# Attention kernel: the units of each batch's third block of row maxima are dealt out two steps ahead of that block's scores in place of one

## The reference, cut to what matters

```python
def _mhsa(X, ln_g, ln_b, Wq, bq, Wk, bk, Wv, bv, Wo, bo):     # X: (2, 1024, 256)
    Xn = (X - mu) * jax.lax.rsqrt(var + EPS) * ln_g + ln_b
    Q = split_heads(Xn @ Wq + bq)                             # 16 heads of 16
    K = split_heads(Xn @ Wk + bk)
    V = split_heads(Xn @ Wv + bv)
    scores = jnp.einsum('bhqd,bhkd->bhqk', Q, K) / jnp.sqrt(jnp.float32(D_HEAD))
    scores = jnp.where(causal, scores, jnp.float32(-jnp.inf))
    A = jax.nn.softmax(scores, axis=-1)
    AV = jnp.einsum('bhqk,bhkd->bhqd', A, V)
    ...
    return AV @ Wo + bo
...
x = _layernorm(x + attention(x))
x = _layernorm(x + mixture(x))    # softmax over 8 of U V x, weights from relu(x W1 + b1) W2 + b2
```

## Time and profile before

| | before |
|---|---|
| median of three runs | 435.47 us |
| lowest, highest | 435.21, 435.81 us |
| the profiled execution's own time | 435.95 us |
| its span, first to last instruction | 434.2 us |
| granted TensorE clock, mean | 0.995 |
| TensorE matmul, busy | 407.1 us (94%) |
| VectorE, busy | 309.1 us (71%) |
| ScalarE, busy | 243.3 us (56%) |
| GpSimd, busy | 74.6 us (17%) |

### The profile page before, as it was taken

One profiled execution on the slowest core, in us unless ns is written; L12 is line 12 of the kernel. 1 busy time (PEld: TensorE's weight loads), 2 busy tenths in 40 slices (PEclk: granted clock), 3 DMA queues, 4 the chain that ended last, 5 costly groups with the idle time before them and its releaser, 6 DMA issues.

```text
span 434.2 us, 7411 instructions
## 1 busy us (share of the span) xinstructions
PE 407.1 (94%) x2563; PEld 214.5 (49%) x2563; DVE 309.1 (71%) x811; ACT 243.3 (56%) x541; POOL 74.6 (17%) x111
## 2 busy tenths in 40 slices
PE   7998899999989989999999999999999998998994
PEld 3545444344333445466768734344334344556783
DVE  5538997798799766528488799789889863214665
ACT  6681555676767666543441265666676857542321
POOL 4430211143121010102230022114212011010000
PEclk9999999999999999999999999999999999999989
DMA  6166760450402000001764045054130000000011
GB/s 194 15 104 93 193 99 15 68 82 7 70 2 98 1 3 0 2 1 31 147 124 64 15 86 91 10 87 63 23 53 3 0 4 0 2 0 2 0 48 49
DMA packets 18452, 21.14 MB, mean 49 GB/s; under 512 B 4976, under 2 KB 11888, under 8 KB 18416
## 3 DMA queue, kind: packets, MB, share of 16 engines
q1 hardware_dynamic: 18365, 20.66, 25.4%
q10 hardware_dynamic: 51, 0.01, 0.0%
HBM read 5.79 MB, written 2.10 MB: 18 GB/s over the span
## 4 chain that ended last, share of the span: by engine, by line
PE 74%; DVE 16%; ACT 6%; issue 2%; DMA 1%; POOL 1%; ACTq 0%; DVEq 0%; POOLq 0%
PE ps L951 17%; PE ps L1066 14%; PE ps L1045 14%; PE ps L1022 10%; DVE mx L822 9%; PE ps L959 8%; PE ps L967 4%; PE ps L942 2%; PE ps L1026 2%; ACT pr L675 2%; PE ps L1136 2%; PE ps L1076 1%; DVE ps L818 1%; ACT stk L596 1%; ACT qk_raw L661 1%
## 5 line engine op out<-in xcount | busy, mean ns | idle before, releaser
L675 ACT ACTIVATE pr<-ps 128x512 f32<-128x512 f32 (+3 forms) x384 | 165.9, 495 | 95.5 <-PE ps L1045 94.0
L822 DVE TENSOR_REDUCE mx<-ps 128x1 f32<-128x512 f32 (+3 forms) x240 | 145.6, 665 | 14.6 <-PE ps L1022 7.4
L1045 PE MATMUL ps<-stq,stk 99*128 99x512 bf16 (+3 forms) x384 | 116.2, 330 | 4.6 <-ACT pr L675 3.3
L1022 PE MATMUL ps<-stk,stq 96*128 96x512 bf16 (+3 forms) x384 | 112.8, 327 | 2.1 <-DVE mx L822 0.9
L587 POOL TENSOR_SCALAR_AFFINE_SELECT pr<-pr 128x512 f32<-128x512 f32 x64 | 40.9, 639 | 253.6 <-ACT pr L675 253.6
L1066 PE MATMUL ps<-pr,va 128*32 128x512 f32 (+3 forms) x768 | 81.8, 498 | 0.0
L1045 PEld LDWEIGHTS ps<-stq,stk 99*128 99x128 bf16 x384 | 34.4, 98 | 90.4 <-ACT pr L675 51.8
L1022 PEld LDWEIGHTS ps<-stk,stq 96*128 96x128 bf16 x384 | 37.5, 98 | 23.5 <-issue 7.7
L818 DVE CUSTOM_DVE_ANT_0 ps<-ps,causal 128x384 f32<-128x384 f32 (+1 forms) x64 | 38.6, 646 | 11.3 <-PE ps L1022 11.3
L1026 PE MATMUL ps<-mask,ident_b 128*128 128x128 bf16 x192 | 35.4, 219 | 0.0
L951 PE MATMUL ps<-u_t,avt 128*128 128x256 f32 x128 | 30.8, 383 | 0.3 <-ACT avt L711 0.2
(11 more groups left out here) (108 smaller groups left out, 389.3 us busy)
## 6 DMA issues: line engine op xcount, KB each, us to landing
stq<-qk_raw SPq DMA_DIRECT2D x32, 96.0 KB, 2.8
stk<-qk_raw SPq DMA_DIRECT2D x32, 96.0 KB, 2.8
x_in<-in_x SPq DMA_DIRECT2D x8, 256.0 KB, 3.5
stq<-qk_raw SPq DMA_DIRECT2D x32, 64.0 KB, 2.4
stk<-qk_raw SPq DMA_DIRECT2D x32, 64.0 KB, 2.4
out_y<-x SPq DMA_DIRECT2D x3, 512.0 KB, 3.0
stk<-qk_raw SPq DMA_DIRECT2D x32, 32.0 KB, 2.4
stq<-qk_raw SPq DMA_DIRECT2D x32, 32.0 KB, 2.1
```

The costliest lines, as they stand in the source:

```text
L675: nc.scalar.activation(probs(b, g, s)[:, j, q0 - c * CHUNK:], act_bank(ev)[:, q0 - c * CHUNK:], ACT.Exp, scale=DH ** -0.5).then_inc(s_act_ ...
L822: nc.vector.tensor_reduce(dst, src, AX.X, ALU.max).then_inc(s_dve_free, 1)
L1022: last = nc.tensor.matmul(bank[:, i * w:(i + 1) * w], q[0:ROWS, t // TPC, j, tile(t % TPC)], k[0:ROWS, k0 // CHUNK, j, 0:w], start=True, s ...
L1045: nc.tensor.matmul(bank[:, q0 - c * CHUNK:], stk[stack_of(b, g)][0:ROWS + PARTS, kt // TPC, j, tile(kt % TPC)], stq[stack_of(b, g)][0:ROWS ...
```

## The change

One number: the third point of the course moves from one step ahead of the third block's first score to two, so from step 7 to step 6. The number of units due there (50) and the last point (step 37, 152 units) stay.

```diff
-    course = [(0, needed[0] + 6), (first_step[1], needed[1] + 12), (first_step[2] - 1, needed[2] + 1), (first_step[-1] - 3, needed[-1])]
+    course = [(0, needed[0] + 6), (first_step[1], needed[1] + 12), (first_step[2] - 2, needed[2] + 1), (first_step[-1] - 3, needed[-1])]
```

## The result

| | before | changed |
|---|---|---|
| median, taken side by side, 16 runs each | 436.03 us | 439.26 us |
| ratio to before, 95% interval | | 1.0065 (1.0042 to 1.0089) |
| profiled execution's own time, span | 435.95, 434.2 | 440.27, 438.2 |
| TensorE, VectorE, ScalarE busy in the profile | 407.1, 309.1, 243.3 | 410.6, 308.6, 243.9 |
| mean granted TensorE clock in the profile | 0.995 | 0.990 |

The change makes the kernel 0.65% slower: 2.8 us by the ratio (its interval is 1.8 to 3.9 us), 3.2 us between the two medians, and 4.0 us between the two profiled executions. The forecast had the sign and gave 1.15 us.

The account below looks back on a forecast made before the run. TensorE (74% of the chain) and VectorE (16%) were taken to bound it in turns, with work moved to where VectorE is full. Batch 0's 0.45 plus batch 1's 0.7 gave 1.15 us, so 436.6 us, range 435.2 to 437.9.

Parts of the forecast that it names:

- Part 2: Steps 9 to 21, new places of rows(2,0) and rows(3,0): 0.3 us lost and 0.3 us gained, 0.75 to 0.8 late at step 26.
- rows(3,0): Rows matmul in step 21: its split moves into step 20, so its wait falls from 0.38 to 0.1 us.
- rows(2,0): Rows matmul now in step 9 with its split: a new wait of about 0.3 us, bounds 0 and 0.6.
- Part 1: Up to the dummies: M55 waits for M51's bank on VectorE, so the dummies start 1.4 us late in each batch.
- Part 3: VectorE's stretch from M114 to split(2,1): M115 starts 0.55 us late; batch 0 ends 0.45 us late, batch 1 0.7.
- The sign given for what would show it: In the profile after, TensorE waits for VectorE at a unit of step 7.
- What comes back at once: After the dummies: 0.5 us for M53 to M55 and 0.15 us of filled wait in step 8, leaving 0.75 a batch.
- the rest is as late: From M115 on VectorE has no idle time, so its 0.55 us delay carries through the stretch.
- waits for banks: Batch 0, when M125 to M134 are wanted: VectorE owes 0.55 us more, giving 0.3 us of waits in the ring of four.
- the loss stays whole: Rival: wait at rows(2,0) is 0.6, that at rows(3,0) stays, VectorE's debt paid after step 29; 437.9 us, chance 0.10.
- The advice on gaps: Rule to start the blocking dependency sooner: alone, both batches would gain their gap at rows(0,1), 0.8 us in all.
- The rival "faster": Three units done early needn't be done later, when VectorE bounds from M114 on: -0.6 and -0.4 us, 434.5 us; chance 0.07.

Follow-up runs that it names:

- Kernel 2: Kernel before with six units in step 7 in place of three, so 56 are issued ahead of step 8; 440.95 us, ratio 1.0089.
- Kernel 1: Changed kernel with one more course point: steps 4 and 5 keep eight units each, but only 53 are issued ahead of step 8; 438.13 us, ratio 1.0049.
- kernel 5: Changed kernel with rows(2,0) and rows(3,0) moved back to the ends of steps 10 and 21; 437.9 us, ratio 0.9992.
- kernel 3: Changed kernel with matmuls on constants in the waits ahead of rows(2,1), 5 in batch 0 and 3 in batch 1; 438.37 us, ratio 1.0049.
- kernels 10 and 12: Changed course, 3 dummies, rows(2,0) and rows(3,0) late, constant matmuls ahead of rows(2,1) (second: batch 0 only, batch 1 rows(2,1) late); 433.47 and 432.18 us.
- kernel 12: Changed course, 3 dummies, rows(2,0) and rows(3,0) late, constant matmuls ahead of rows(2,1) in batch 0, rows(2,1) late in batch 1; 432.18 us, ratio 0.9883.
- kernel 7: Kernel before with 6 dummies ahead of step 8 in place of 13; 434.77 us, ratio 0.9954.
- kernels 5 and 6: Changed kernel with rows(2,0) and rows(3,0) late (437.9 us, ratio 0.9992); changed kernel with 6 dummies in place of 13 (436.44 us, ratio 1.0011).

## Why the prediction was right or wrong

The direction and most of the mechanism were right. The step that failed is Part 2, the places of the rows: rows(3,0) was put down as a gain of 0.3 us a batch and its new place cost 0.31, for a bank of ScalarE's ring that the forecast didn't count, and rows(2,0) was put at 0.3 and cost 0.65 and 0.45. The smaller misses are Part 1 (0.2 us a batch) and what Part 3 made of it in batch 1.

**Part 1, the dummies 1.4 us late: the size was right, the releaser was not.** Measured 1.59 and 1.57. The step said that M55 waits for M51's bank and that TensorE, at 0.22 us a unit, keeps up otherwise. Kernel 2 shows that limit by itself, 1.57 us. In the changed kernel itself TensorE was late on its own account: the step counted what TensorE needs for the units of steps 4 to 6, but not that being held at VectorE's pace leaves the values of step 5 and all of steps 6 and 7 undone, 6.1 us from M49 on. In steps 4 and 5 it did wait for VectorE's banks, 1.0 us in all; so it kept up with VectorE, but not with its own scores and values. Kernel 1 has 0.95 us from that alone. The sign given for what would show it, a wait for VectorE at a unit of step 7, is missing from the profile. That the size came out near is in part luck, since two limits lie within 0.02 us of each other here.

**What comes back at once: right.** The forecast left 0.75 us; step 9 is 1.59 late with three units of 0.66 more in front, so 0.93. The 0.2 is the difference of Part 1.

**Part 2, the rows' places: one size low, one sign wrong.** rows(2,0) cost 0.65 and 0.45 us by kernel 5, forecast 0.3 with 0.6 as a bound. At rows(3,0) the forecast took a gain of 0.3, and the new place cost 0.31 against kernel 5. The split's wait of 0.38 did go, to 0.08. But the forecast asked only for the split of this event, not for the bank it takes in ScalarE's ring, which hangs on an exponential behind ScalarE's drain of the values. Even with the rows back at the end of the step that wait is 0.46 us (kernel 5). The rows matmul stands 2.30 us into step 21 before the change and 2.21 in kernel 5, so of the 0.3 about 0.1 was to be had. This term, 0.6 us wrong in each batch, is the largest that both batches share.

**Part 3, the second stretch of VectorE: right in kind, the size follows from Part 2.** M115 was indeed what hangs on the values: VectorE starts it 1.7 us late in batch 0 and split(2,1) comes later with it. With 0.8 us of delay at step 26 the forecast had 0.55; the true delay, 2.15 less the unit in front, is 1.2 us more, which makes 1.7. In batch 1 the stop ahead of rows(2,1) stayed, 0.82 us where it was 0.79, as the forecast's "the rest is as late" says, so nothing was absorbed: 1.77 at step 26 became 1.89, where the forecast went from 0.8 to 0.7. In batch 0 the v_t split behind split(2,1) gave its 0.6 us and a little more (in kernel 3, where the clock is full, the delay goes from 2.14 at step 26, 0.17 of it M114, to 1.13 at step 30). For waits for banks after it the forecast had 0.3; in kernel 3 the trace shows one of 0.20 us, at 132.22, and the delay grows by 0.24 from step 30 to the end.

**The clock: missing.** The forecast had listed the stop of 1.96 us as room, shrinking to 1.2 (measured 1.23), and had a full clock there in the profiled execution of before. The fall cost 1.2 us in the profiled run of the changed kernel; without it the 4.0 us between the two profiles would be 2.8. It isn't shown to be a loss of the change itself. Low clocks were about as common in the changed kernel (8 of 16) as in the kernel before (14 of 34). What sets it off stays open.

**The sum.** Forecast 1.15. Measured, without the fall of the clock: 1.37 + 1.88 = 3.25 (kernel 3), which lies in the ratio's interval of 1.8 to 3.9 us. At step 26 the forecast had 0.8, and 1.98 and 1.77 were measured (2.15 and 1.94 less M114). Missing are 0.2 from Part 1, and from Part 2 0.95 in batch 0 (0.35 at rows(2,0), 0.6 at rows(3,0)) and 0.75 in batch 1, which is all of it up to there. Behind step 26 batch 0 did 0.26 better than forecast and batch 1 0.2 worse. The measured ratio puts the changed kernel at 438.3 us where the range ended at 437.9. The case "the loss stays whole", at 10%, is the nearest, but only in part for its reasons: rows(2,0) did cost 0.6 in batch 0, but the wait at rows(3,0) didn't just stay at 0.38, and VectorE's debt after step 29 came to 0.24 us.

**The advice on gaps.** The gap of 0.41 us at rows(0,1) did go, as the Trainium skill (Perfetto Trace Analysis, section Optimization Strategy) would have it, and its place was taken by work: TensorE's chain has no stop from 61.0 to 67.1. The advice bears out only together with what the gap's neighbour, the dummies, still has to cover. With that cut (kernels 10 and 12) the earlier dependency paid.

**The rival "faster"** was wrong for the edit alone and half right in kernel 12: the earlier maxima are worth something once the dummies don't stand in their way.

## What to carry to other kernels

When work is moved ahead of a point where one engine waits for another, ask two things: what the waiting engine has left undone meanwhile, and what filler was put there for the old order. An event moved between others takes its buffers along, so each ring it draws on has to be counted anew, not only the semaphore it waits for. And compare two profiles only after looking at the granted clock stretch by stretch: here 1.2 of 4.0 us were that. The same holds for medians: lay the mean clocks of the executions beside them before a gain is put down to the order.

## What the runs showed of the hardware that was not expected

TensorE's clock fell to the lower of its levels (1.2 GHz) in the middle of a kernel in which TensorE is busy 94% of the time, 1.1 us after a stop of 1.23 us: matmuls of 128 columns went from 0.06 to 0.11 us apart, and the granted clock was 0.50 from 129.3 to 132.7 us. It doesn't do so in every execution: 14 of 34 executions of the kernel before had a mean clock of 0.991 or less. With matmuls on constants in the stop it was one of 12, but with the stop left as it was and fewer dummies at step 8 (kernel 7) it was one of 10 as well. In kernels 5 and 6 a stop of the same length had a full clock behind it. What decides isn't known. A DMA of 12 KB from SBUF to SBUF took 2.4 us from its issue to the start of the matmul that waited for it (kernel 7), with the 16 DMA engines 29% busy.
